# GpSimd's share of the last batch's outer products: four z of all channels, one scalar multiply each

## The reference, cut to what matters

```python
e = jnp.stack([tbl_0[ids[:, 0]], ..., tbl_15[ids[:, 15]]], axis=1)   # 2048 x 16 x 256
xk = x                                    # x = e
for i in range(3):
    z = jnp.einsum('bfe,bge->bfge', x, xk).reshape(B, 16 * 16, 256)
    z = jnp.einsum('bcl,oc->bol', jnp.swapaxes(z, 1, 2), Ws[i]) + bs[i][None, :, None]
    z = jnp.sum(jax.nn.relu(z), axis=-1)  # B x 16
    outs.append(z)
    xk = jnp.broadcast_to(z[:, :, None], (B, 16, 256))
h = jnp.concatenate([outs (48 columns), dense_ctx (16 columns)], axis=1)
h = jnp.maximum(h @ W_top1 + b_top1, 0.0)
h = jnp.maximum(h @ W_top2 + b_top2, 0.0)
y = h @ W_top3
```

## Time and profile before

| | |
|---|---|
| median of three executions | 604.71 us |
| lowest and highest | 603.44, 604.80 us |
| the profiled execution, first to last instruction | 612.3 us |
| of it between the median and the span | 7.6 us |
| DVE busy | 551.6 us (90%) |
| ACT busy | 496.0 us (81%) |
| PE busy | 482.5 us (79%), mean granted clock 0.939 |
| POOL busy | 470.3 us (77%) |

### The profile page before, as it was taken

One profiled execution on the slowest core, in us unless ns is written; L12 is line 12 of the kernel. 1 busy time (PEld: TensorE's weight loads), 2 busy tenths in 40 slices (PEclk: granted clock), 3 DMA queues, 4 the chain that ended last, 5 costly groups with the idle time before them and its releaser, 6 DMA issues.

```text
span 612.3 us, 10749 instructions
## 1 busy us (share of the span) xinstructions
PE 482.5 (79%) x4014; PEld 195.0 (32%) x4014; DVE 551.6 (90%) x326; ACT 496.0 (81%) x1427; POOL 470.3 (77%) x354
## 2 busy tenths in 40 slices
PE   6124887768786888878879779898988879888988
PEld 5001232323232333323233223333333323333345
DVE  1046999999999999999999999999999999899995
ACT  1001449799989989899989899999989898999876
POOL 6771068887888888888888888888888888885911
PEclk9556999999899989999999999989999888989998
DMA  3530012221222222222222212222122221120000
GB/s 99 154 106 26 1 51 57 67 68 47 60 70 61 61 57 66 69 65 58 61 62 70 64 57 61 62 70 68 56 60 61 69 70 56 50 70 1 2 1 0
DMA packets 14332, 35.41 MB, mean 58 GB/s; under 512 B 5493, under 2 KB 5879, under 8 KB 14266
## 3 DMA queue, kind: packets, MB, share of 16 engines
q0 software_dynamic: 12288, 33.57, 19.2%
q1 hardware_dynamic: 1994, 1.17, 0.7%
HBM read 34.71 MB, written 0.01 MB: 57 GB/s over the span
## 4 chain that ended last, share of the span: by engine, by line
DVE 36%; POOL 22%; issue 21%; ACT 9%; PE 9%; another core or an unknown queue 2%; DMA 1%; ACTq 0%; DVEq 0%
DVE prod L398 29%; POOL x_rows L323 13%; POOL intra L337 9%; DVE outer L446 5%; ACT outer L599 4%; PE z_ps L790 4%; ACT xt L536 1%; PE t_ps L753 1%; ACT sq L544 1%; ACT outer L589 1%; PE turn_ps L854 1%; PE zs_ps L891 1%; DVE outer L464 1%; ACT relu L555 1%
## 5 line engine op out<-in xcount | busy, mean ns | idle before, releaser
L398 DVE TENSOR_TENSOR prod<-t_ps,xt 128x2048 f32<-128x2048 f32 x190 | 420.7, 2279 | 34.6 <-issue 25.5
L323 POOL DMA_INDIRECT x_rows<-in_tbl,ids_sb x256 | 246.7, 964 | 71.8 <-issue 68.2
L599 ACT ACTIVATE outer<-outer,bias_sb 128x256 f32<-128x256 f32 x487 | 241.4, 512 | 5.2 <-DVE outer L446 5.2
L337 POOL TENSOR_TENSOR intra<-xt 128x1024 f32<-128x1024 f32 (+4 forms) x90 | 210.2, 2354 | 43.1 <-PE z_ps L790 35.1
L790 PE MATMUL z_ps<-prod,w_sb 128*32 128x512 f32 x1520 | 190.3, 614 | 33.5 <-DVE prod L398 27.0
L536 ACT ACTIVATE xt<-t_ps 128x512 f32<-128x512 f32 x128 | 75.1, 602 | 69.3 <-issue 29.1
L446 DVE TENSOR_TENSOR outer<-y_ps,z_all 128x1536 f32<-128x1536 f32 (+2 forms) x66 | 110.5, 1717 | 7.4 <-ACT outer L589 4.7
L753 PE MATMUL t_ps<-ident,x_rows 128*128 128x128 f32 x512 | 82.7, 292 | 36.6 <-issue 23.2
L599 ACT ACTIVATION_READ_ACCUMULATOR outer<-outer,bias_sb 128x1 f32 x487 | 99.7, 205 | 0.0
L753 PEld LDWEIGHTS t_ps<-ident,x_rows 128*128 128x128 f32 x512 | 57.1, 145 | 99.1 <-issue 81.5
L790 PEld LDWEIGHTS z_ps<-prod,w_sb 128*32 128x32 f32 x1520 | 46.5, 111 | 122.2 <-issue 98.3
(11 more groups left out here) (61 smaller groups left out, 202.7 us busy)
## 6 DMA issues: line engine op xcount, KB each, us to landing
x_rows<-in_tbl,ids_sb POOLq DMA_INDIRECT x256
w_sb<-in_w SPq DMA_DIRECT2D x1, 512.0 KB
feat<-in_dense SPq DMA_DIRECT2D x1, 128.0 KB
w_sb<-in_w SPq DMA_DIRECT2D x1, 128.0 KB
ids_sb<-in_ids SPq DMA_DIRECT2D x1, 120.0 KB
ident<-in_identity SPq DMA_DIRECT2D x1, 64.0 KB, 1.9
...
```

The source lines that it names most:

```text
L323: pool.indirect_dma_start(out=x_rows[:, par, f, :], out_offset=None, in_=tables[f], in_offset=bass.IndirectOffsetOnAxis(ap=ids_sb[:, NF * ...
L337: pool.tensor_tensor(intra[:, pair, :, q:, at:at + n], x[:, :, q:, 0:n], x[:, :, q:, d * P:d * P + n], ALU.mult).then_inc(intra_done, 1)
L398: dve.tensor_tensor(prod[:, m % PROD_RING, half, :].rearrange("p (f g s) -> p f g s", f=QF, g=QF), t_ps[:, tbank(b, q, half), :, :].unsque ...
L599: act.activation(outer[:, o // OP, o % OP, :], outer[:, o // OP, o % OP, :], ACT.Relu, bias=bias12_sb[:, layer - 1, o:o + 1], accum_out=z_ ...
```

## The change: what it does

POOL's part of `outer` in the last batch is turned by a quarter. Before, POOL multiplies channels 12 to 15 for all 16 g, in one `tensor_tensor` of 1024 values per partition for each layer, and DVE multiplies channels 0 to 11 in three pieces of 1024. After, POOL multiplies g 12 to 15 for all 16 channels, in four `tensor_scalar` of 256 values for each layer, whose scalar is z[g] of each partition; they write every 16th value of a channel. DVE multiplies g 0 to 11 for all channels in four pieces of 768. `y_last` therefore holds all channels, and its copy on ACT has 512 columns in place of 128.

Every channel now has values from both engines. So each of the sums in the last batch waits for its DVE piece and for POOL's four instructions of that layer (`pool_outer` at 4 times the layer). Before, the sums of channels 0 to 11 waited for DVE alone and those of 12 to 15 for POOL alone.

The tensor `zeros`, the third operand of `vector_sum`, shrinks from 256 columns to one that is read with a step of zero, and its memset with it. Batches before the last are as they were.

```diff
--- before.py
+++ after.py
@@ -83,13 +83,13 @@
         zs_sb = sb("zs_sb", [P, P])
         yt_sb = sb("yt_sb", [P, QF, P])
         z_all = sb("z_all", [P, 2, NL, NF])
-        y_last = sb("y_last", [P, QF, GROUPS, 2, LAST_OP])
+        y_last = sb("y_last", [P, QF, GROUPS, 2, NF])
         outer = sb("outer", [P, PIECES, OP, NF * NF])
         feat = sb("feat", [KH, NB * P])
         h1 = sb("h1", [P, M1, MC])
         h2 = sb("h2", [P, M2, MC])
         y_row = sb("y_row", [1, MC])
-        zeros = sb("zeros", [P, NF * NF])
+        zeros = sb("zeros", [P, 1])
         ids_sb = sb("ids_sb", [P, NB * NF], I32)
         w0_sb = sb("w0_sb", [P, HALVES, 2, GR])
         w12_sb = sb("w12_sb", [P, HALVES, GR])
@@ -200,19 +200,15 @@
 
         def slices(b, layer):
 
-            return SLICES if (b, layer) < (LAST - 1, 2) else 0
+            return 0 if (b, layer) == (LAST - 1, 2) else SLICES
 
         def op(b):
 
             return LAST_OP if b == LAST else OP
 
-        def vector_channels(b):
-
-            return NF - LAST_OP if b == LAST else NF
-
         def piece(b, layer, o):
 
-            return 2 * PIECES * b + vector_channels(b) // op(b) * (layer - 1) + o // op(b)
+            return 2 * PIECES * b + NF // op(b) * (layer - 1) + o // op(b)
 
         def mlp_slot(frame, kind):
 
@@ -355,13 +351,11 @@
                     pool.wait_ge(z0_moved, NB)
                 pool.wait_ge(z_ready, z_count(LAST, layer - 1))
                 pool.wait_ge(vector_summed, vector_count(LAST, layer - 1))
-                o = NF - LAST_OP
-                y = y_last[:, :, :, layer - 1, :].rearrange("p f c o -> p o (f c)")
-                pool.tensor_tensor(
-                    outer[:, o // OP, o % OP:o % OP + LAST_OP, :].rearrange("p o (f g) -> p o f g", f=NF),
-                    y.unsqueeze(3).to_broadcast([P, LAST_OP, NF, NF]),
-                    z_all[:, LAST % 2, layer - 1, :].unsqueeze(1).unsqueeze(1).to_broadcast([P, LAST_OP, NF, NF]),
-                    ALU.mult).then_inc(pool_outer, 1)
+                y = y_last[:, :, :, layer - 1, :].rearrange("p f c o -> p (f c) o")
+                out = outer[:, :, :, :].rearrange("p k i (f g) -> p f (k i) g", f=NF)
+                for g in range(NF - SLICES, NF):
+                    pool.tensor_scalar(out[:, :, :, g], y, z_all[:, LAST % 2, layer - 1, g:g + 1], None,
+                                       ALU.mult).then_inc(pool_outer, 1)
 
             pool.wait_ge(ids_first, 16)
             gather(0, 0, NF)
@@ -432,7 +426,7 @@
                     return
                 n = op(b)
                 m = NF - slices(b, layer)
-                if m < NF:
+                if m < NF and b < LAST:
                     dve.wait_ge(sliced, SLICES * (2 * b + layer))
                 else:
                     if layer == 1:
@@ -450,20 +444,19 @@
                     ALU.mult).then_inc(outer_done, 1)
 
             def outer_pieces(b, layer):
-                for o in range(0, vector_channels(b), op(b)):
+                for o in range(0, NF, op(b)):
                     outer_piece(b, layer, o)
 
             def vector_sum(b, layer, first, last):
 
                 dve.wait_ge(zeroed, 1)
                 for o in range(first, last):
-                    if o < vector_channels(b):
-                        dve.wait_ge(outer_done, piece(b, layer, o) + 1)
-                    else:
-                        dve.wait_ge(pool_outer, layer)
+                    dve.wait_ge(outer_done, piece(b, layer, o) + 1)
+                    if b == LAST:
+                        dve.wait_ge(pool_outer, SLICES * layer)
                     dve.scalar_tensor_tensor(
                         outer[:, o // OP, o % OP, :], outer[:, o // OP, o % OP, :],
-                        bias12_sb[:, layer - 1, o:o + 1], zeros[:, :], ALU.add, ALU.max,
+                        bias12_sb[:, layer - 1, o:o + 1], zeros[:, :].to_broadcast([P, NF * NF]), ALU.add, ALU.max,
                         accum_out=z_all[:, b % 2, layer, o:o + 1]).then_inc(vector_summed, 1)
 
             def tail_vector_move(g, i):
@@ -596,6 +589,8 @@
                 for o in range(first, min(last, NF - vector_sums(b, layer))):
                     if o == first or o % op(b) == 0:
                         act.wait_ge(outer_done, piece(b, layer, o) + 1)
+                        if b == LAST:
+                            act.wait_ge(pool_outer, SLICES * layer)
                     act.activation(outer[:, o // OP, o % OP, :], outer[:, o // OP, o % OP, :], ACT.Relu,
                                    bias=bias12_sb[:, layer - 1, o:o + 1],
                                    accum_out=z_all[:, b % 2, layer, o:o + 1]).then_inc(z_ready, 1)
@@ -610,7 +605,7 @@
             def copy_y_last():
 
                 act.wait_ge(y_turned, NB)
-                act.activation(y_last[:, :, :, :, :], y_ps[:, :, :, :, NF - LAST_OP:NF], ACT.Copy).then_inc(y_copied, 1)
+                act.activation(y_last[:, :, :, :, :], y_ps[:, :, :, :, :], ACT.Copy).then_inc(y_copied, 1)
 
             def mlp_move(t, i):
                 act.wait_ge(turn_ready, mlp_turn(t, i) + 1)
```

## The result

The changed kernel took 613.42, 613.71, 617.32 and 609.46 us, median 613.57, against a median of 604.75 us of the kernel before in four runs (603.44 to 609.29). The ratio is 1.0129, with a 95% interval from 1.0068 to 1.0191: slower, by 8.8 us between the medians, where 1.2 us had been forecast and 608.0 was the upper end of the range.

What follows compares the result with a forecast made beforehand. The last batch's chain from ACT's first layer 1 sums through PE's second layer was taken to bind, not DVE. Waits of 1.02 and 0.18 us made 1.20, so 604.71 became 605.9 us; range 604.3 to 608.0.

Steps and rivals of the forecast that it cites:

- the cost of POOL's new instruction: POOL's tensor_scalar of 256 values in the last batch: 0.56 us each, bounds 0.18 and 0.73, four in 2.24.
- rival A: POOL's instruction is as dear as its two-stream form, 0.73 us: loss 2.55, time 607.3; chance 0.26.
- B: POOL's instruction is quick, up to 0.45 us: loss 0.41 to 0.58, time 605.2; chance 0.18.
- Wider copy: ACT's copy to y_last grows from 258 to 602 ns, so z_all, DVE and POOL go 0.34 us later.
- DVE's pieces: DVE's four products of 768 span 3.56 us in place of 3.49 for three of 1024, +0.07 per layer.
- ACT's wait in layer 1: ACT's first sum waits for POOL until 593.64 in place of 592.62, delaying PE's second layer and layer 2: +1.02 us.
- ACT's wait in layer 2: ACT's sums start another 1.06 us later, mostly hidden behind PE before form_feat and tail_y(0): +0.18 left.
- 8x - 3.28: Loss in us from x = 0.52 up, x being one POOL instruction's time and D four in a row.
- DVE's sums: In both layers they wait for POOL too, but DVE's own pieces end later: no cost unless four take over 3.5 us.
- signs of being wrong: ACT's first sum on time, DVE waiting for POOL, or DVE's or POOL's instructions growing from writing the same rows of outer.
- zeros: The early memset and the sums' third operand read with a step of zero were priced at nothing.
- Rival C: PE's longer idle time puts all of its second layer at half clock: +4.2 us, time 608.9; chance 0.03.

Runs made afterwards that it cites:

- probe: The changed kernel with ten more POOL instructions behind its sums, into dead memory, run for their lengths alone; a single execution of 587.73 us.
- before_plain: The kernel before, without an edit, run for a profile against the same kernel; means 610.7 and 610.8 us, ratio 1.0002.
- after_again: The changed kernel once more without an edit, against the kernel before; means 609.3 and 606.4 us, ratio 1.0045.
- after_fourth: The changed kernel again without an edit, against the kernel before; means 580.55 and 574.51 us, ratio 1.0106.

## Why the prediction was wrong

The step that failed is the one I called "the cost of POOL's new instruction". I took 0.56 us, 2.24 for four, where 4.27 was measured, and bounded it above by the 0.73 of the 256-value `tensor_tensor`, on the ground that one stream is cheaper than two. It isn't: the change's form takes 1.07, and in the probe it took 1.13 alone where `tensor_tensor` with the same input and output took 0.64. The nearest row was of another operation, and I used it as a ceiling. An operation that no row shows has no ceiling from a row of another one. The outcome lies past rival A, which I gave 0.26: right in mechanism, wrong in its price: it had 0.73 for the instruction, 607.3 for the whole. Two smaller slips: the range's ends, B less half a microsecond and A with as much above, come to 604.6 and 607.8 and not 604.3 and 608.0; neither would have held the result.

Weighing the Trainium skill misled in the same direction. "GPSIMD Engine Reference", section 4.1, has one-input work as roughly line-rate. That fits the copy here, 0.40 us for 256, about what the earlier trace rows make of 256 values on DVE (0.15 + 0.27, an estimate), and not `tensor_scalar` (0.93). Its section 7 rule on steps of more than 8 bytes is one for reads; turned on the writes it gave 0.80 as an estimate (D near 3.2). Here the stepped output costs 0.11 from one instruction to the next, and the dense form is already past 0.80.

Point by point:

1. *Wider copy.* Right: 0.32 by the starts, 0.34 forecast.
2. *DVE's pieces.* Right: 3.55 us, 3.56 forecast.
3. *ACT's wait in layer 1.* Right in place, wrong in size: ACT begins 4.36 - 1.60 + 0.32 = 3.1 us later, 1.02 forecast. With D = 4.27, D - 1.22 gives 3.05.
4. *ACT's wait in layer 2.* The same: 4.32 - 1.22 = 3.1, 1.06 forecast. Of it 0.88 was to be hidden behind PE, and PE's idle time of 1.3 us shows that the cover was used up. The prediction's formula for the loss, 8x - 3.28, which is 2D - 3.28, gives 5.26 us; the stage and the copy together measure 5.1 + 0.3 = 5.4. But this cover is there only in executions of the kernel before in which the clock fell. In before_plain it did not, ACT's sums released `form_feat`, and the stage was 0.8 shorter. Against such an execution the same sum without the cover is 2D - 2.40 = 6.1 us, and the stages and the copy measure 26.4 - 20.5 + 0.3 = 6.2. The steadiest session had 6.0; in which state its executions of the kernel before were is not known. So I had taken the state of one profiled execution for that of all; at the forecast D of 2.24 this alone would have made the loss 2.1 us and not 1.2.
5. *DVE's sums.* I had written that DVE waits if four take over 3.5 us: they take 4.27 and DVE waits 0.9. It did not add to the loss, since ACT's nine sums end later than DVE's seven (594.5 and 592.5). DVE waiting for POOL was one of my signs of being wrong, and it came; the other, both engines growing as they write into the same rows, did not (the probe).
6. *zeros.* Right: a sum of DVE takes 0.48 in the earlier trace rows and after.

*Rival C*, the clock, I had at +4.2 us with a chance of 0.03. Its premise came true: PE idled for 4.04 us ahead of the second layer, and the clock was 0.50 for more than half of the layer. It took 7.7 us (601.76 - 594.08) against 7.0 before and cost nothing, since PE was done at 602.8 and waited for ACT. What I had not seen is the tail, where I held that PE's time would not change. In before, the clock was at half speed for the first half of the second layer in one profile and not in another (21.3 and 20.5). The changed kernel adds a second idle stretch, ahead of the tail, and in two of its four profiles the clock fell there, for 3.3 us; in the probe's it did as well. That the fall differs between executions is shown. In the three with the fall PE had stood still for 1.72 to 1.75 us, in the two without for 1.26 and 1.17; from after_again:

```profile
604.91 0.27 PE L841 MATMUL turn_ps<-ident,z_all 128*48 128x128 f32 x1 [1.73 <-issue]
```

In these three the second layer had also ended sooner, after an early stretch at 0.50 that began about a microsecond sooner. Which of the two decides, if either does, is not shown.

The account for the session with the least spread: 0.3 for the copy and 26.4 - 20.5 = 5.9 for the stage make 6.2, or 5.4 if the clock fell in before, against 6.0 measured. For the first session, 7.9, a late fall in part of the runs and the spread of four runs have room for the rest. The 2.9 of after_again, 0.8 to 4.7 us by its interval, lies below the stage's own loss of 5.1 to 5.9. The spread ahead of the last batch is the only candidate, and nothing shows it; this stays open.

## What to carry to other kernels

Before an operation moves to GpSimd in another form, time that form on the chip: here a product of 256 values by a per-partition scalar took 1.13 us as `tensor_scalar`, and the same product as a broadcast `tensor_tensor` 0.64. Where a slow helper has a share of a layer, give it whole units that are consumed last. The same 4 us of POOL were nearly free when only the last channels waited, and cost 5 when a quarter of every channel was POOL's. And a term that hides another is checked in more than one execution before it is counted on: the 0.88 us that PE was to hide was there in one profile of the kernel before and not in the other.

## What the runs showed beyond that

The time ahead of the last batch varies by far more than the change. With the same kernel before, sessions had means from 574 to 611 us. DVE's timelines show where. A run of six products in the second batch began at 62.60 in the profile before and at 32.47 in that of after_fourth, 30 us sooner:

Before:

```profile
41.49 2.29 DVE L398 TENSOR_TENSOR prod<-t_ps,xt 128x2048 f32<-128x2048 f32 x1 [8.14 <-issue]
...
52.00 8.88 DVE L398 TENSOR_TENSOR prod<-t_ps,xt 128x2048 f32<-128x2048 f32 x4 [6.41 <-ACT xt L536]
...
62.60 13.27 DVE L398 TENSOR_TENSOR prod<-t_ps,xt 128x2048 f32<-128x2048 f32 x6
```

After_fourth:

```profile
32.47 13.27 DVE L392 TENSOR_TENSOR prod<-t_ps,xt 128x2048 f32<-128x2048 f32 x6
```

The products themselves take the same 13.27 us in both; it is the waits ahead of them, in the first batch, that differ: DVE idled for 17.37, 8.14 and 6.41 us ahead of its products of the profile before, and for 2.44 in that of after_fourth. POOL reached the last batch's layer 1 at 591.02 and at 552.48, so 8 us more were lost in between. What makes the first batch's waits so different is not shown. A change of some microseconds at the end of such a kernel is read from the length of its stage, not from the span.
